# Two blocks of the MLP ahead of the output projection, and the low halves dealt out anew, in a one-core attention and MLP kernel

## What is computed

```python
h0 = _layernorm(x)                                  # rows normalised, no gain
# _L0_attn_ref(h0, ...):
h1 = layernorm(h0, ln1_g, ln1_b)
q, k, v = h1 @ wq, h1 @ wk, h1 @ wv                 # 16 heads of 16
kv  = einsum('bshd,bshe->bhde', elu(k) + 1, v);  z = sum(elu(k) + 1, axis=1)
a   = (elu(q) + 1) @ kv / ((elu(q) + 1) . z + 1e-6)
y   = h0 + a @ wo
h2  = layernorm(y, ln2_g, ln2_b)
y2  = y + lookup_gelu(h2 @ w1) @ w2                 # w1 256 x 1024, w2 1024 x 256
# grid = round(h/0.1) clipped to int8; gelu of the grid value
x2  = x + y2
out = x2 + layernorm(x2) @ CB.T * (SCB / 127) + bias
```

## Time and profile before

| | |
|---|---|
| median of 3 runs | 569.27 us |
| the profiled execution | 567.73 us |
| its span, first to last instruction | 565.9 us |
| TensorE busy | 94% |
| VectorE busy | 80% |
| ScalarE busy | 70% |
| GpSimd busy | 61% |
| mean granted TensorE clock | 0.994 of full speed |

### The profile page before, as it was taken

How to read it: one execution, slowest core, us unless ns; L and a number is a source line. 1 busy time by engine, 2 the same in 40 slices (tenths; PEclk the granted TensorE clock), 3 DMA queues, 4 the chain that set the end, 5 groups by cost and what they waited for, 6 DMA issues and landing times.

```text
span 565.9 us, 11319 instructions
## 1 busy us (share of the span) xinstructions
PE 533.6 (94%) x3610; PEld 485.9 (86%) x3610; DVE 451.6 (80%) x1059; ACT 396.5 (70%) x656; POOL 344.9 (61%) x336
## 2 busy tenths in 40 slices
PE   6899999899989899999999999999999999999885
PEld 6789998798878788989898898988989889898775
DVE  5899998899777588886978879788787878879636
ACT  2587874656558587876968768687776878768760
POOL 3344336142222578687686877768787786877654
PEclk9899998999999999999999999999999999999999
DMA  7423111211101011010201202012020210200001
GB/s 267 143 75 111 58 54 39 69 43 38 38 23 38 1 39 43 32 75 0 74 37 37 74 2 74 37 37 74 0 74 0 74 49 25 74 0 39 37 1 77
DMA packets 11419, 29.47 MB, mean 52 GB/s; under 512 B 2048, under 2 KB 4864, under 8 KB 11392
## 3 DMA queue, kind: packets, MB, share of 16 engines
q1 hardware_dynamic: 9472, 28.32, 14.1%
q10 hardware_dynamic: 1920, 0.79, 0.6%
HBM read 20.71 MB, written 8.39 MB: 51 GB/s over the span
## 4 chain that ended last, share of the span: by engine, by line
PE 68%; DVE 15%; issue 8%; POOL 4%; ACT 2%; DMA 2%; DVEq 0%; POOLq 0%; SPq 0%; ACTq 0%
PE psum L1021 61%; PE psum L1039 5%; DVE bn_stats_b L684 3%; DMA f_arena<-in_L_attn_x_dram 2%; DVE f32r_arena L837 2%; PE psum L1060 2%; POOL f32r_arena L383 2%; DVE f32r_arena L829 2%; DVE mean_var L691 1%; DVE bn_stats L684 1%; DVE n_and_ones L711 1%; ACT f_arena L612 1%; DVE f_arena L711 1%; ACT f32r_arena L614 1%; DVE f_arena L874 1%
## 5 line engine op out<-in xcount | busy, mean ns | idle before, releaser
L1021 PE MATMUL psum<-w_hi,f32r_arena 128*128 128x256 f32 x1280 | 174.3, 282 | 4.7 <-POOL f32r_arena L383 3.0
L1021 PEld LDWEIGHTS psum<-w_hi,f32r_arena 128*128 128x128 f32 x1280 | 164.1, 188 | 14.0 <-issue 5.8
L1021 PE MATMUL psum<-f32r_arena,w_hi 128*128 128x512 f32 x512 | 141.1, 402 | 1.4 <-issue 1.4
L383 POOL TENSOR_TENSOR f32r_arena<-f_arena,f32r_arena 128x512 fp32r<-128x512 f32 x64 | 85.5, 1336 | 82.6 <-ACT f32r_arena L614 46.4
L601 ACT ACTIVATE grid_index<-psum,w_bias_in_steps 128x512 int8<-128x512 f32 x128 | 87.2, 681 | 50.8 <-PE psum L1021 50.7
L1021 PEld LDWEIGHTS psum<-f32r_arena,w_hi 128*128 128x128 f32 x512 | 88.1, 188 | 14.8 <-issue 1.6
L612 ACT ACTIVATE f_arena<-grid_index 128x512 f32<-128x512 int8 x128 | 80.9, 632 | 24.7 <-POOL f32r_arena L383 16.4
L614 ACT ACTIVATE f32r_arena<-grid_index 128x512 fp32r<-128x512 int8 x128 | 79.2, 619 | 0.0
L1021 PE MATMUL psum<-f32r_arena 128*128 128x256 f32 (+1 forms) x384 | 70.7, 334 | 2.5 <-DVE f32r_arena L723 1.9
L1021 PEld LDWEIGHTS psum<-f32r_arena 128*128 128x128 f32 x384 | 56.8, 195 | 7.9 <-issue 3.0
L829 DVE TENSOR_TENSOR f32r_arena<-f_arena,f32r_arena 128x512 fp32r<-128x512 f32 x64 | 57.9, 905 | 1.2 <-ACT f32r_arena L614 1.2
(11 more groups left out here) (117 smaller groups left out, 872.0 us busy)
## 6 DMA issues: line engine op xcount, KB each, us to landing
f_arena<-in_L_attn_x_dram SPq DMA_DIRECT2D x32, 512.0 KB, 3.3
out_dram<-f_arena SPq DMA_DIRECT2D x15, 512.0 KB, 2.7
f_arena<-in_L_attn_w_dram SPq DMA_DIRECT2D x2, 1024.0 KB, 12.6
out_dram<-f_arena SPq DMA_DIRECT2D x2, 256.0 KB, 2.1
phi_q<-in_L_attn_wk_dram ACTq DMA_DIRECT2D x1, 256.0 KB, 4.7
phi_q<-in_L_attn_wq_dram SPq DMA_DIRECT2D x1, 256.0 KB, 4.9
phi_q<-in_L_ffn_CB_dram SPq DMA_DIRECT2D x1, 256.0 KB, 7.2
phi_q<-in_L_attn_wo_dram SPq DMA_DIRECT2D x1, 256.0 KB, 8.0
```

Of the source, the lines that this page charges most:

```text
L383: nc.gpsimd.tensor_tensor(t_lo[m % SLOTS], tf[m % 2], t_hi[m % SLOTS].bitcast(F32), ALU.subtract).then_inc(s["t_lo_p"], 1)
L1021: return nc.tensor.matmul(out_, lhs, rhs, start=start, stop=stop, skip_group_check=True)
```

## The change

On TensorE, block 4's w1 pass and block 1's w2 pass stand ahead of the wo product; they stood behind it. On ScalarE, block 1's gelu and block 2's quantise stand ahead of the attention rows' high half. VectorE makes the low halves of blocks 0, 1, 2 and 5, GpSimd those of 3, 4, 6 and 7: block 2 and block 3 have changed places. VectorE's low half of block 1 goes ahead of the attention rows' low half, and that of block 2 goes between the third norm and the y2 sum. GpSimd makes block 7's low half between the second and the third of the four instructions of `first_norm`. Chunk 0 gets nearly the same order as the others. Nothing else is changed, and no instruction is added or removed in work or size.

```diff
-        LOW_V, LOW_P = (0, 1, 3, 5), (2, 4, 6, 7)
+        LOW_V, LOW_P = (0, 1, 2, 5), (3, 4, 6, 7)
 # GpSimd
-            def first_norm(c, p, turn):
+            def first_norm(c, p, turn, low_of=None):
 ...
                 for j in range(TT):
+                    if j == 2 and low_of is not None:
+                        mlp_low(low_of, 7)
                     i = nc.gpsimd.tensor_scalar(tm(yb)[:, j], tm(x2[p])[:, j], ...
 ...
-                    mlp_low(i, 2)
+                    mlp_low(i, 3)
 ...
                 if nn:
-                    first_norm(i + 2, p, turn + 1)
-                if main:
+                    first_norm(i + 2, p, turn + 1, low_of=i)
+                elif main:
                     mlp_low(i, 7)
 # ScalarE
                 if main:
                     mlp(i, 0)
                     quantise(i, 1)
-                if is_chunk(i, 0):
                     gelu(i, 1)
                     quantise(i, 2)
                 if nxt:
                     wait(a, s["cb_done"], i + 1)
                     high(i + 1, "attn_turned", SB2, "s_hi_a")
-                if is_chunk(i, 0):
+                if main:
                     gelu(i, 2)
                     mlp(i, 3)
-                else:
-                    gelu(i, 1)
-                    mlp(i, 2)
-                    mlp(i, 3)
 # VectorE
                 if is_chunk(i, 0):
                     attend(1, 1)
+                if main:
                     mlp_low(i, 1)
                 if nxt:
                     attn_low(i + 1)
                 if is_chunk(i, 0):
                     turned_sums(1, SA)
-                    mlp_low(i, 3)
-                else:
-                    mlp_low(i, 1)
                 if prv:
                     v.wait_ge(s["mv3_ready"], i)
                     normalise(i - 1, xp, mv3, r3, "pow3", "n3_ready")
+                if main:
+                    mlp_low(i, 2)
                 if nxt:
                     first_residual(i + 1)
-                if main and not is_chunk(i, 0):
-                    mlp_low(i, 3)
 # TensorE
                     else:
                         ...
                         down(i, 0)
+                    up(i, 4)
+                    down(i, 1)
+                    if is_chunk(i, 0):
+                        turn_sums(1, SA)
                     if nxt:
                         attention_out(i + 1, not exact)
-                    if not is_chunk(i, 0):
-                        down(i, 1)
-                        up(i, 4)
```

More of the change, by code:

```diff
@@ L1298, in body @@
                         turn_attention(1)
-                        down(i, 1)
-                        up(i, 4)
-                        turn_sums(1, SA)
                     else:
```

## The result

| | before | after |
|---|---|---|
| median, first comparison (4 runs each) | 569.45 us | 560.72 us |
| ratio to before | | 0.984 (0.980 to 0.988) |
| a second comparison, on one chip (11 and 6 runs) | 568.0 us | 561.18 us |
| ratio to before | | 0.988 (0.986 to 0.990) |
| the profiled execution | 567.73 us | 560.22 us |

The change makes the kernel 1.2% to 1.6% faster. The profiled executions differ by 7.5 us, the spans by 7.4. The forecast was 561.8 for the median and 560.3 for the profiled execution, which took 560.22.

The account below looks back on a forecast made before the run. TensorE, busy 94%, bounds the kernel and loses by waiting for wo; 14 chunks gain 0.80 - 0.21 - 0.12 = 0.47 each, 6.6, and 6.6 + 0.9 + 0.2 - 0.3 = 7.4 gives a median of 561.8 us. Range 556.5 to 566.5.

Parts of the forecast that it names:

- The wo wait of 0.80: TensorE's wo product waits for VectorE's attention low half; each of 14 chunks loses 0.80 us, which the change removes.
- The clashes: With D the start of block 7's w2 pass: GpSimd sums delay VectorE's block 0 and 1 low halves; wo stalls 0.21.
- The rival that priced it at the full 0.68: Blocked VectorE low halves of blocks 0 and 1 each pay 0.14 more, 3.9 us in all, 565.7; chance 0.07 within 0.27.
- The cb product's new wait: On TensorE, the cb product waits for the third product's low half (L841): a new stall of 0.12 a chunk.
- Turn 2: TensorE wants the second norm at D+15.89, which ends near D+15.75: 0.15 to spare instead of 1.46, nothing lost.
- Block 7's low half: On GpSimd between the passes of y, it ends 0.6 before its w2 pass; at its old place about 0.5 late.
- Chunk 0: The 0.16 wait on block 7's low half in the first chunk goes: 0.2 us gained.
- The last but one chunk: No attention passes hide the later block 6 chain there: 0.3 us charged as a loss.
- The last chunk: Block 2's w2 pass no longer waits 0.72 for GpSimd's low half, which moves to VectorE: 0.9 gained with the refill.
- The full gain: Rival: GpSimd's output sum ends before VectorE's block 0 low half; TensorE loses at most 0.12; 557 to 559.5, chance 0.18.
- The gain was not eaten: Rival: block 0 and 1 low halves wait in full or the chain lengthens; stalls 0.47 to 0.8, 563.6 to 568.5, chance 0.27.
- The slower case: Rival: GpSimd's block 3 low half begins later than D+8.98, turn 2 stalls; some 575 us or more, chance 0.05.

Follow-up runs that it names:

- The last experiment: Changed kernel with wo between block 4's w1 and block 1's w2 pass, and ScalarE's high half, then block 2's quantise, before block 1's gelu: 555.74 us, ratio 0.977.

## Why the prediction was right, point by point

- *The wo wait of 0.80 goes.* Right. The last experiment, in which wo doesn't wait, has a period of 23.24, which is 24.04 - 0.80.
- *The clashes: the two sums on GpSimd push the two low halves back.* Right, and the times are those of the sum: L420 ends at D+2.76 (2.8), block 0's low half at D+3.32 (3.36), block 1's at D+6.13 (6.17), L834 at D+7.45 (7.49), wo starts at D+7.60 (7.64), 0.20 late (0.21). Both clashes were confirmed by taking away one side of each.
- *How long the one that comes second is blocked.* The low half ended 0.56 behind the output sum's end (386.80 - 386.24) and 0.55 behind that of the sum into xz (389.61 - 389.06), like the 0.54 of the earlier trace rows. The Trainium skill (SBUF — State Buffer, Who interferes with whom) has the second one block fully; the trace agrees that it blocks, but the blocked low half needs less than its 0.68 behind the other's end. The rival that priced it at the full 0.68 falls.
- *The cb product's new wait.* Right: 0.08 (0.12).
- *The size of a small wait.* Here a term was mis-sized. "A new stall of 0.21" and "a new stall of 0.12" count only the late start. A group of 16 matmuls that had to wait can also take longer to the next group. In the changed kernel wo takes 1.97 in 12 of 14 chunks (391.08 to 393.05), and the cb product in 13 (397.76 to 399.73); without a wait both take 1.88 or 1.89 (387.68 to 389.56 and 395.14 to 397.03 in the last experiment). That adds 0.17. So 0.28 + 0.17 = 0.45 are given back in this chunk (by the periods 23.67 - 23.24 = 0.43), not 0.33. The two runs with a short sum agree: only the cb product waits in them, and their periods are 0.15 above 23.24. The sum left the same effect out of what goes, where it is smaller: in the kernel before, wo takes 1.96 in 9 of 14 chunks and 1.89 in 5, 0.05 on the mean, so 0.85 goes and not 0.80. Over the 13 chunks of the table the gain is 0.42 each instead of 0.47, 0.7 us less than forecast.
- *Turn 2.* Right. The norm ends at D+15.96 (forecast D+15.75), turn 2 starts at D+16.25, directly behind the cb product, with no wait for the norm. Block 3's low half starts at D+8.96, as the rival needed it not to be later.
- *Block 7's low half.* It ends at 382.81, 0.67 ahead of its w2 pass (forecast 0.6), and at its old place it is 0.40 late (forecast 0.5). That it also pushes the output sum into VectorE's low half was in the sum, but not as its price: the experiment shows it net, 0.2 a chunk.
- *Chunk 0.* Mis-sized: 0.78 instead of 0.2. Of it 0.13 comes from the first stage and so has nothing to do with the change. Turn 2 is 0.32 earlier (187.03 to 186.71), and block 7's w2 pass, which waited 0.16, does not wait: 195.25 to 194.55. I had counted the wait alone. That block 3's low half no longer precedes the y2 sum on VectorE is the likely cause of the earlier turn 2; no run takes it apart.
- *The last but one chunk.* Right: from wo to block 7's w2 pass 16.93 before and 15.37 now; less 1.88 would be 15.05, so 0.32 is lost (forecast 0.3), and the row at 524.79 shows a wait of 0.78 for GpSimd.
- *The last chunk.* The size is right (0.88), a place is not: block 2's w2 pass no longer waits for GpSimd, but the transposes ahead of it wait 1.40 for the third norm, which waits for the power on GpSimd. That is no new loss: before, block 1's w2 pass waited 0.96 there (537.16) and the transposes 0.48 (539.72), 1.44 together, for a norm that hung on the power in the same way.

```profile
531.90 1.38 DVE L817 TENSOR_SCALAR f_arena<-f_arena,mean_var,rstd 128x256 f32<-128x256 f32 x4 [1.26 <-POOL rstd L364]
...
533.34 1.09 PE L1034 MATMUL psum<-ident,f_arena 128*128 128x128 f32 x8 [1.40 <-DVE f_arena L817]
```

- *The rivals.* The full gain (557 to 559.5) did not come, since the output sum still runs at D+2.34, where VectorE starts block 0's low half. The gain was not eaten either (563.6 and more), but what is given back, 0.45 a chunk, comes close to the 0.47 at which that rival begins; the mechanism is another one, the longer group and not the low half's full 0.68. The slower case, turn 2 as the stall, stayed away. Another way to be slower, which is no rival in the prediction, is near: if GpSimd's low half runs beside the third norm, the kernel is slower than before (574.63 us).

What stays open: the exchange of blocks 2 and 3 was tried only as a whole, so whether another pair would do better isn't known, and GpSimd's late chain from block 4's low half on was not shortened in any run.

## What to carry to other kernels

When a product is moved behind other passes to hide its wait, compute again for each engine when every later low half or bank is wanted, also those that belong to the passes in between: here three companions of the move were worth 16, 3 and 3 us (the exchange, ScalarE's order, block 7's place, each taken back alone), against 7 to 9 for the whole. A wait that seems idle can be what keeps two engines out of each other's way, so price its removal by what then runs side by side. And a wait of a group of 16 matmuls costs its idle time and some 0.2 more: 0.16 until the first one starts (0.80 late for 0.64 idle, 0.20 for 0.03) and up to 0.08 within the group.

## What the runs showed of the hardware

- A VectorE instruction with a single tensor as input is blocked by GpSimd too: the third norm, float32 and SBUF to SBUF, takes 1.38 alone, 2.42 beside a GpSimd low half of 1.29, and 4.35 beside two GpSimd instructions of 3.75 together. I had counted only instructions with two such inputs as open to this, and so let GpSimd's work run beside it in the experiment with block 2's low half earlier. The Trainium skill (SBUF — State Buffer, Who interferes with whom) names `tensor_scalar` among the operations that can contend in a two-port mode; the trace agrees in its effect, and shows no mode.
- The blocking goes both ways: GpSimd's sum of 1024 columns takes 2.39 where it comes first (383.85) and 2.85 when it meets VectorE's low half (386.21), a low half 1.27 to 1.30 alone and 1.57 at 392.44.
- A group of 16 matmuls that starts late takes 1.96 or 1.97 to the next group in most chunks and 1.89 in the others (12 to 2 for wo in the changed kernel, 9 to 5 in the kernel before), and 1.88 or 1.89 without a wait. What decides between the two is not shown.
- TensorE's granted clock fell while it waited 4.72 us for the norm: it was 0.50 from 544 to 550 us, and eight transposes took 1.97 instead of 1.09.
